# A fused decoder layer on one core: context values projected at the end of the attention, a new order of prologue and last tile, and sixteen spare matmuls

## The reference

```python
x = x + attn(_layernorm(x), W_dq, W_uq, W_qr, W_dkv, W_ukv, W_kr, W_o, q_ln, kv_ln)  # causal, 16 heads of 16, low-rank q and kv
x = x + xattn(_layernorm(x), ctx_2048, ctx_2048, Wh, wg, wo, gn)
x = x + ffn(_layernorm(x), gate, w_gate_up, w_down, shared)                          # 16 experts, top 2, and a shared one
...
def xattn(x, k, v):                      # 2 heads of 128; x, k, v are [8, 128, 256]
    Q, K, V = xh @ Wh, kh @ Wh, vh @ Wh  # per head; k and v are the same context
    masked = (Q @ K.T / sqrt(128)) * decay
    A = maximum(abs(masked.sum(axis=0)), 1.0)     # summed over the 8 batches
    O = A @ V                                     # per batch
    return (relu(x @ wg) * groupnorm(O)) @ wo
```

## Time and profile before

| | us |
|---|---|
| median of 3 runs | 262.43 |
| lowest and highest | 260.69, 265.61 |
| the profiled execution's own time | 264.52 |
| span of its trace | 262.4 |
| PE, DVE, ACT, POOL busy in the span | 239.2, 148.8, 129.0, 92.3 |

### The profile page before, as it was taken

The page is one execution under the profiler, slowest core; times in us unless marked ns, Lnnn a source line. Parts: engine busy times, 40 slices in busy tenths (PEclk is TensorE's granted clock), DMA queues, the critical chain, the costliest instruction groups (busy, mean ns, idle before and its releaser), DMA issues.

```text
span 262.4 us, 5169 instructions
## 1 busy us (share of the span) xinstructions
PE 239.2 (91%) x1628; PEld 176.7 (67%) x1628; DVE 148.8 (57%) x451; ACT 129.0 (49%) x465; POOL 92.3 (35%) x109
## 2 busy tenths in 40 slices
PE   8768879899999999968787999989999999999995
PEld 6437356666675677847565878756777777777783
DVE  1456827798788877532789569845233232232275
ACT  1124787898898978830052522503433443333340
POOL 2110201111211111010266101464777777777461
PEclk9959999999999999988999999999999999999999
DMA  7999987500000620000001300032232333334396
GB/s 209 238 344 346 368 202 189 152 5 4 4 0 2 224 91 0 4 0 2 0 0 40 122 0 1 5 100 80 71 111 100 102 100 100 106 102 112 104 317 227
DMA packets 20852, 28.10 MB, mean 107 GB/s; under 512 B 2833, under 2 KB 17819, under 8 KB 20827
## 3 DMA queue, kind: packets, MB, share of 16 engines
q1 hardware_dynamic: 16683, 19.01, 24.1%
q0 software_dynamic: 2976, 8.13, 10.2%
q10 hardware_dynamic: 1167, 0.65, 1.0%
HBM read 21.62 MB, written 6.16 MB: 106 GB/s over the span
## 4 chain that ended last, share of the span: by engine, by line
PE 54%; issue 13%; ACT 11%; DMA 9%; DVE 8%; POOL 2%; SPq 1%; ACTq 1%; POOLq 0%; DVEq 0%
PE bank L882 13%; PE bank L894 8%; ACT pr_s L991 7%; PE bank L813 7%; PE bank L522 5%; DMA lnkv_s<-in_ln_kv 4%; PE bank L863 3%; DMA x_s<-expert_out 2%; PE bank L873 2%; PE bank L527 2%; PE bank L570 2%; PE bank L555 2%; PE bank L645 1%; PE bank L498 1%; ACT prT L981 1%
## 5 line engine op out<-in xcount | busy, mean ns | idle before, releaser
L991 ACT ACTIVATE pr_s<-bank,mx 128x128 f32<-128x128 f32 x128 | 45.3, 383 | 9.6 <-DVE mx L1221 9.0
L882 PE MATMUL bank<-gu_s,bxT 128*128 x124 | 41.7, 460 | 0.2 <-DVE bxT L1544 0.2
L1550 DVE TENSOR_TENSOR pr_s<-bank,pr_s 128x176 f32<-128x176 f32 x31 | 10.6, 341 | 51.7 <-ACT pr_s L1150 50.9
L483 POOL DMA_INDIRECT expert_out<-by,prT x31 | 31.1, 1004 | 15.1 <-ACT by L981 7.7
L478 POOL DMA_INDIRECT qx_s<-ffn_in,prT x31 | 30.1, 972 | 14.5 <-issue 8.2
L981 ACT ACTIVATE prT<-bank 128x512 f32<-128x512 f32 (+1 forms) x63 | 30.7, 497 | 2.2 <-PE bank L570 1.2
L894 PE MATMUL bank<-dn_s,prT 88*128 x124 | 31.7, 379 | 0.0
L991 ACT ACTIVATION_READ_ACCUMULATOR pr_s<-bank,mx 128x1 f32 x128 | 28.6, 223 | 0.0
L882 PEld LDWEIGHTS bank<-gu_s,bxT 128*128 128x128 f32 x124 | 21.2, 190 | 7.2 <-issue 0.4
L570 PE MATMUL bank<-tab,pr_s 128*128 128x128 f32 x128 | 19.5, 275 | 5.4 <-ACT prT L981 2.8
L1221 DVE TENSOR_REDUCE mx<-bank 128x4 f32<-128x512 f32 x32 | 20.4, 682 | 5.9 <-PE bank L555 5.8
(11 more groups left out here) (192 smaller groups left out, 428.8 us busy)
## 6 DMA issues: line engine op xcount, KB each, us to landing
gu_s<-in_w_gu SPq DMA_DIRECT2D x8, 704.0 KB, 8.7
dn_s<-in_w_dn SPq DMA_DIRECT2D x4, 704.0 KB
qx_s<-in_ctx_in SPq DMA_DIRECT2D x2, 512.0 KB, 10.5
ffn_in<-x_s SPq DMA_DIRECT2D x4, 256.0 KB, 2.1
cv_s<-expert_out SPq DMA_DIRECT2D x4, 256.0 KB, 4.3
x_s<-expert_out SPq DMA_DIRECT2D x4, 256.0 KB, 6.0
out<-x_s SPq DMA_DIRECT2D x7, 128.0 KB, 4.0
gu_s<-in_x_t SPq DMA_DIRECT2D x1, 768.0 KB, 12.4
```

The lines of the kernel that those rows point to most:

```text
L483: pool.indirect_dma_start(expert_out[:], bass.IndirectOffsetOnAxis(ap=idx[:, 1, k:k + 1], axis=0), by[:, k % RB, :], None).then_inc(dma_sc ...
L882: last = mm(bank[2 + i % 2][:, 0:2 * I], bxT[:, i % 2, k, :], gu_s[:, k, bass.ds(e, 1), :], start=k == 0, stop=k == KD - 1)
L991: last = nc.scalar.activation(pr_s[:, n % 2, h, :], score_bank(n)[:, h * T:(h + 1) * T], ACT.Exp, bias=mx[:, n % 4, h:h + 1], accum_out=de ...
L1550: V.tensor_tensor(bh[:, i % 2, :], bank[2 + i % 2][:, I:2 * I], bs[:, i % 2, :], ALU.mult).then_inc(dve_hidden, 1)
```

## The change

The context values' four groups leave the prologue and the loop and go behind the loop, one by one between `cross_scores`; `cross_mix(q)` now waits for group q. The context's buffer `cT` therefore has to live longer and moves from `qx_s` into the part of `gu_s` for experts 0 to 7 (second half of the contraction); their two weight transfers are issued only once the context values are made. The layer-norm weights go as columns into the constant table, so that ACT's queue holds one table transfer in place of four. Tile 1 of `x_s` is loaded ahead of `wht_s`. In the prologue `qk_transpose(0)` goes ahead of `latent_transpose(1)`, DVE's `q_out(0)` ahead of `latent_normalize(1)`, and the variances of tiles 4 to 7 are computed in tile 0 of the loop. In the last tile the cross scores are spread over its steps, the last transpose has a bank of its own, DVE's `denominators(7)` goes ahead of `x1_variance(6)`. Sixteen products of the constant matrix `mean_w` with itself, which nobody reads, stand at four places: 4 ahead of `latent_transpose(0)`, 3 and 4 around `mix_transpose(0)`, 5 ahead of `ffn_transpose(0)`.

```diff
-        lnq_s = sb("lnq_s", [128, 2])
-        lnkv_s = sb("lnkv_s", [KPH, 2, 2])
+        lnq_s = tab[:, C_LN:C_LN + 2]
+        lnkv_s = tab[0:KPH, C_LN + 2:C_LN + 6].rearrange("p (k n) -> p k n", k=2)
...
-        cT = qx_s[:].rearrange("p b k t -> p (b k t)")[:, 0:B * D].rearrange("p (h b t) -> p h b t", h=XH, b=B)
+        cT = gu_s[:, 1, 0:E // 2, :].rearrange("p e n -> p (e n)")[:, 0:B * D].rearrange("p (h b t) -> p h b t", h=XH, b=B)
...
-        probs_bank = lambda n: bank[3 if n % NC == 2 else 2]
-        ctx_key_bank = lambda g, h: bank[(6, 3)[h] if g else h]
-        ctx_value_bank = lambda g, j: bank[3 if g else j]
+        probs_bank = lambda n: bank[0 if n == NC * B - 1 else 3 if n % NC == 2 else 2]
+        ctx_key_bank = lambda g, h: bank[6 if g else h]
+        ctx_value_bank = lambda g, j: bank[1 + j]
+        rden_half = lambda b: bank[6 if b < B - 1 else 5][:, D:2 * D]
...
             sp.dma_start(x_s[:, 0:1, :], xv[:, 0:1, :]).then_inc(ld_x[0], 16)
+            sp.dma_start(x_s[:, 1:2, :], xv[:, 1:2, :]).then_inc(ld_x[1], 16)
             sp.dma_start(wht_s, wh_t.rearrange("h p n -> p h n")).then_inc(ld_wh_t, 16)
             sp.dma_start(cT[:, :, 0:4, :], ctx_in[:, :, 0:4, :]).then_inc(ld_ctx0, 16)
             sp.dma_start(wkv_s[:], w_kv.rearrange("(k p) n -> p k n", p=KPH)).then_inc(ld_w_kv, 16)
-            sp.dma_start(x_s[:, 1:2, :], xv[:, 1:2, :]).then_inc(ld_x[1], 16)
...
-            for k, e in ((0, 0), (0, 4), (0, 8), (0, 12), (1, 0), (1, 4)):
+            for k, e in ((0, 0), (0, 4), (0, 8), (0, 12)):
...
+            sp.wait_ge(pe_ctx_values, B // 2)
+            expert_weights(1, 0)
+            expert_weights(1, 4)
...
             def qk_transpose(b):
-                if b == 1:
-                    pe.wait_ge(act_ctx_keys, 4)
-                if b == 2:
-                    pe.wait_ge(act_ctx_values, 4)
...
+            def keep_busy(where, n):
+                for k in range(n):
+                    mm(where[:, 0:T], mean_w[:], mean_w[:], start=True, stop=True)
...
             ctx_keys(0, 0)
-            pe.wait_ge(ld_identity, 16)
+            keep_busy(bank[7], 4)
+            pe.wait_ge(ld_table, 16)
             latent_transpose(0)
             ctx_keys(0, 1)
             pe.wait_ge(ld_w_q, 16)
             pe.wait_ge(ld_w_kv, 16)
             queries(0)
             keys_values(0)
+            qk_transpose(0)
             latent_transpose(1)
-            ctx_values(0, 0)
-            qk_transpose(0)
-            ctx_values(0, 1)
             pe.wait_ge(ld_table_b, 16)
-            pe.wait_ge(act_ctx_values, 2)
+            pe.wait_ge(act_ctx_keys, 2)
...
                 if i == 0:
                     ctx_keys(1, 0)
-                    ctx_keys(1, 1)
-                if i == 1:
-                    ctx_values(1, 1)
...
                 if i == B - 1:
                     gates(2, 0)
-                    gates(2, 1)
...
-                if i == 0:
-                    ctx_values(1, 0)
+                if i == B - 1:
+                    gates(2, 1)
+                    cross_scores(0)
                 if tiles(i + 2):
                     latent_transpose(i + 2)
+                if i == 0:
+                    ctx_keys(1, 1)
...
+            cross_scores(1)
             prob_transpose(NC * B - 1)
+            cross_scores(2)
+            weigh_values(NC * B - 4)
+            weigh_values(NC * B - 3)
+            weigh_values(NC * B - 2)
             rden_transpose(B - 1)
-            for c in range(NC):
-                weigh_values(NC * (B - 1) + c)
+            weigh_values(NC * B - 1)
+            cross_scores(3)
+            out_project(B - 1)
             cross_transpose(B - 2)
-            cross_scores(0)
-            cross_scores(1)
-            out_project(B - 1)
-            for b in range(2, B - 1):
-                cross_scores(b)
+            ctx_values(0, 0)
+            cross_scores(4)
+            cross_scores(5)
+            ctx_values(0, 1)
+            cross_scores(6)
             cross_transpose(B - 1)
-            cross_scores(B - 1)
+            ctx_values(1, 0)
+            cross_scores(7)
+            ctx_values(1, 1)
             gates(3, 0)
...
             def cross_mix(q):
                 pe.wait_ge(dve_decayed, 1)
+                pe.wait_ge(act_ctx_values, q + 1)
...
+            keep_busy(bank[5], 3)
             mix_transpose(0)
+            keep_busy(bank[5], 4)
             mix_transpose(1)
...
             pe.wait_ge(act_last_gates, 1)
+            keep_busy(bank[5], 5)
             ffn_transpose(0)
...
-            act.dma_start(tab[:, C_ID:C_ID + 128], table[:, C_ID:C_ID + 128]).then_inc(ld_identity, 16)
-            act.dma_start(tab[:, C_ROPE:C_DECAY], table[:, C_ROPE:C_DECAY]).then_inc(ld_table, 16)
-            act.dma_start(lnq_s[:], ln_q).then_inc(ld_ln, 16)
-            act.dma_start(lnkv_s[:], ln_kv.rearrange("(k p) n -> p k n", p=KPH)).then_inc(ld_ln, 16)
+            act.dma_start(tab[:, 0:C_DECAY], table[:, 0:C_DECAY]).then_inc(ld_table, 16)
...
-            act.wait_ge(ld_ln, 32)
+            act.wait_ge(ld_table, 16)
             latents_out(0)
...
             latent_variance(1)
+            q_out(0)
             latent_normalize(1)
-            q_out(0)
             qk_out(0)
-            x_variances(2, B)
+            x_variances(2, 4)
...
+                if i == 0:
+                    x_variances(4, B)
+                if i == B - 1:
+                    denominators(i)
                 if tiles(i - 1):
                     x1_variance(i - 1)
```

72 lines of the change are left out of this document (37 added, 35 removed).

## The result

The changed kernel takes **252.79 us** in the median (252.54 to 254.34, 4 runs), the kernel before, beside it on the same chip, 262.41 us (260.69 to 265.61, 4 runs). The ratio is 0.967, with a 95% interval of 0.960 to 0.973: faster by 3.3%. The forecast was 253. The profiled execution took 252.71 us, its span 250.7.

A forecast was written before the change was run, and what follows sets the result against it. Prologue and end of the attention, both at half clock, were taken as the stretches to gain in; 4.6 + 3.0 + 2.0 - 0.1 = 9.5 us gave 252.9, rounded to 253 us, range 250 to 257.5.

The forecast's parts named there:

- Term 1: Prologue: without the small load and at the high clock masks start at about 19.1 instead of 23.73, gain 4.6 us.
- So I take the high clock: Prologue: with the spare products the clock stays high, so queries and keys take 2.3 us instead of 4.4.
- Term 2: Loop: tiles 0 and 1 lose context work, 1.8 and 1.2 us, gain 3.0 us, between 1.6 and 3.5.
- the price of tile 0: Loop, tile 0: ACT gets ahead by 1.75 us, so 1.8 us shorter, bounds 0.6 and 2.3.
- Term 3: End of the attention: TensorE becomes the bound, waits are filled, gain 2.0 us, 1.0 to 2.6.
- Term 4: Behind the mix: spare products add 0.1 us; the two late weight transfers stay hidden.
- From the profile to the median: Whole kernel: profiled execution lay 2.1 us above the median, so 255.0 profiled becomes 252.9 in the medians.
- A: Prologue: the clock falls all the same, gain 2.5 in place of 4.6 us, 255 us; chance 0.15.
- B: Prologue: the weights were the real wait, queries(0) at 15.0 to 15.5, 253.6 to 254.1 us; chance 0.15.
- C: Loop and end: context work was hidden where it was, is open where it goes, 257 us; chance 0.12.
- D: Last tile: the clock falls in its chain, costing up to 14 us, 263 to 267 us; chance 0.03.
- E: TensorE's order: the order does nothing; given no size and no chance of its own.

The follow-up runs named there:

- the table kernel: The kernel before with the layer-norm weights in the constant table and nothing else changed: 262.48 us, ratio 1.001.
- values back: The changed kernel with the four groups of context values back in the prologue and tiles 0 and 1: 258.04 us, ratio 0.983.
- table and spare four: The kernel before with the layer-norm weights in the constant table and four spare products ahead of latent_transpose(0): 262.67 us, ratio 0.999.

## Why the prediction was right, and which steps were not

The time was right to 0.2 us, the sum behind it less so. My reading of the earlier trace rows and of the tiles' periods held, and the three largest pieces of the change are each borne out by a kernel that lacks them; the sizes of two terms and the reason for a third were off.

**Term 1** gave 4.6 us, measured 4.74, with the starts as forecast (14.3 and 14.00, 16.6 and 16.28, 19.1 and 18.99). Its parts were not as I put them. Of the 4.74, 1.6 us come from the value groups (their kernel's masks at 20.57), and the table with the full clock brings 23.73 to 20.28 in the table kernel's profile. Most of that is the half clock of the one execution of before: with the small loads and the full clock there, the kernel before with sixteen products has its masks at 21.14, on another chip. In the medians the table alone is worth nothing, and as small loads in the changed kernel the weights cost nothing either (4.28 us from the first keys to `queries(0)`, against 4.29). Nor does the new order of the prologue bring anything by itself: from `ctx_keys(0, 0)` to the masks it is 10.85 us with the values back, and 10.71 in the table kernel with the old order. "So I take the high clock", for the sake of the four spare products, is the step that failed: the high clock came, and it comes without them too.

**Term 2** was forecast at 3.0 us and measured 4.38, above my upper bound of 3.5. The step that failed is the price of tile 0, 1.8 us: I counted what ACT would no longer have to do at one place, and didn't see that ACT, once early, would only wait longer for the values' group in front of its last exponentials (0.31 us in before, 2.06 in the kernel with the values back). The bound of 2.3 us, down to the period of tile 2, was passed for the same reason. I gave DVE's split of the variances nothing; it was worth 0.78. Tile 1, 10.8, came out at 10.97. Tile 2, which I had left out of the account, became 0.17 us shorter; the four tiles from there to the last take 42.39 us in both kernels.

**Term 3** was forecast at 2.0 us and measured 2.43, within its bounds. From the end of `gates(2, 0)` (98.90 + 1.13 = 100.03) to the mix it is 14.2 us, against 14.8 forecast and 16.78 before; from start to start 15.33 against 125.78 - 108.01 = 17.77. The account was right: the values fill waits (TensorE idle 1.90 us without them, 0.04 with them), the order is worth 1.3 to 1.5 us, and the half clock is gone. That last piece is more than one execution's luck: all four profiles with the old last tile (before, table only, table and spare four, before with all sixteen) have a half-clock stretch in it, and none of the ten profiles of the changed kernel and its variants has one between 92 and 126 us. Either the filled waits or the new order seem to be enough, as the kernels that lack one of the two have none there; one profile of each is little to go by.

**Term 4** was 0.1 us; the transposes' starts behind the mix are 0.1 us earlier than before (4.41 and 4.49 us after the mix's start). I gave the products behind the mix no gain; all sixteen brought 0.6% in the kernel before, and in the changed kernel none is shown.

**From the profile to the median.** I carried the 2.1 us by which the profiled execution of before lay above its median over to the changed kernel. The sum in spans was 2.3 us too small, and this correction 2.2 us too large, as the changed kernel's executions mostly have no low stretch (252.71, 252.86 and 252.54 at 0.999 to 1.000, 254.34 at 0.992). The two errors cancelled, so the hit on the median is partly luck.

**The 9.6 us at equal clock.** Sorting single executions by clock separates the steps from the clock. Without a low stretch the kernel before took 260.03 us (at 1.000, the only such execution of 51 in the three groups) and its twin with the table 259.98 (0.998); the changed kernel takes 252.5 to 252.9. So some 7.3 us are shorter work and waits, and the other 2.3 us of the medians are low stretches that most executions of before have and most of the changed kernel have not. Of the 7.3 us, the values are worth 4.7 (their kernel at 1.000), the order of the end 1.5 and the split of the variances 0.7 to 0.8: together 7.0. This takes for granted that the three add up across chips, and single executions scatter at equal clock too, by 0.6 us in the kernel without the four products and by 1.4 in that without any. The 0.3 us left are all there is for the table, the order of the prologue, the earlier load of tile 1 of `x_s`, the second context keys and the rest, most of which no kernel here has alone.

**The rivals.** A did not come about where I had put it, under the queries and keys; in the profiles of two variants the low clock comes behind the first masks, at a cost of 1.6 to 1.7 us in tile 0 (11.48 and 11.55 us against 9.89), while the sum for its case was 2.1. B fell, though by little: in the changed kernel ACT's `ckvT` releases `queries(0)` at 14.00, but in the kernels with the values back and with the variances in one piece the last to come is `wkv_s`, at 14.01 and 14.04. So the weights land at about the moment at which they are needed and cost nothing. Its support from the earlier trace rows was misread: in the list that it comes from, the 704 KB of `dn_s` have no landing either, and no row shows on how many queues `wkv_s` ran. C fell on both counts, and most clearly: the values were open where they were, at 5.6 us for four groups, and mostly hidden where they went, at 1.1 us. D didn't come about; the end ran at the full clock in all ten profiles. E falls with the kernels that have the values back and the old order of the end.

## What to carry to other kernels

When independent work stands in a loop, price its move by the waits that stand in front of it and behind it in every queue it passes, ACT's and TensorE's both, and not by its own duration: four groups of 1.06 us cost 5.6 us in one place and 1.1 us in another. When the profiled execution lies above its median, find out what in it is above (here stretches at half the clock) before carrying the difference over to the changed kernel. Where a part is worth less than 1%, compare single executions of equal clock, and count a shift in one profile from a landmark ahead of the change: the start of the first keys scattered by 0.7 us between profiles, more than the small loads were ever worth.
